# Masked scores: the mask of unlisted keys moves into TensorE's accumulation, and the weights are applied in SBUF

## The chip, the cores and the metric

The kernel runs on one core of one Trainium2 chip. The metric is the device time of one execution in microseconds (us). The kernel before takes 1881.87 us, the median of 3 runs (1881.48 to 1882.13).

The core's engines run side by side, each with an instruction queue of its own: TensorE (PE; its weight loads are PEld), VectorE (DVE), ScalarE (ACT), GpSimd (POOL), and SyncE (SP), which issues most DMA transfers. They wait for each other through semaphores.

## The reference, cut to what matters

Two attention layers over x (2 batches, 1024 tokens, 256 channels, 16 heads of 16) are chained, and a recurrent mixer with a mixture-of-experts feed-forward block follows. The change is in the first of the two:

```python
lam = LAMBDA_MAX * jnp.exp(-ALPHA * u_prev.reshape(Bb))
use_sparse = lam >= SPARSE_THRESHOLD
scores = jnp.einsum('bhqd,bhkd->bhqk', Q, K) * scale
prior_bias = jnp.where(prior_mask[:Ss, :Ss], 0.0, -1.0).astype(x.dtype)
bias = lam[:, None, None, None] * prior_bias[None, None]
dense_out = jnp.einsum('bhqk,bhkd->bhqd', jax.nn.softmax(scores + bias, axis=-1), V)
s_scores = jnp.einsum('bhsd,bhskd->bhsk', Q, K[:, :, idx]) * scale
s_scores = jnp.where(prior_index_mask[:Ss][None, None], s_scores, -jnp.inf)
sparse_out = jnp.einsum('bhsk,bhskd->bhsd', jax.nn.softmax(s_scores, axis=-1), V[:, :, idx])
out = jnp.where(use_sparse[:, None, None, None], sparse_out, dense_out)
```

A query's list of 32 keys may name a key more than once. The kernel therefore computes all scores densely, takes the exponential, and multiplies it with a weight: how often the query lists the key (sparse), or the exponential of the prior's bias (dense).

## The kernel before

**Jobs and units.** The two attentions are sixteen jobs of four heads each (`JOBS`). Jobs 0 to 7 belong to the first attention (`JOBS[n][0] == 0`, the prior one): batch 0, then batch 1, four jobs each. Jobs 8 to 15 are the causal attention. A prior job has 32 units. A unit is one block of 128 keys by 512 queries for two heads: a score tile of 128x1024 f32 in PSUM. `place` gives a unit's half, key block and pair of heads. There are 256 prior units.

**What a unit goes through.** TensorE writes its scores into one of two PSUM tiles (`SC`, the tiles `wide`), two bf16 matmuls of 512 columns (L1867). Then there are two ways, chosen by `to_pool` from the unit's number in its group of eight:

- Units 0, 1, 3, 4, 6 (`POOL_UNITS`, 160 in all): ScalarE copies the scores to SBUF with a Relu that limits them (L1277) and so frees the PSUM tile, takes the exponential from SBUF to SBUF (L1279), and GpSimd multiplies with the weight table (L1085), both its inputs being in SBUF.
- Units 2, 5, 7 (96 in all): ScalarE takes the exponential inside PSUM (L1271), and VectorE takes the minimum with a large number and multiplies with the weights (L1607), reading the scores from PSUM and the weights from SBUF. Only this frees the PSUM tile.

The limits in both ways are there because the scores of unlisted keys can be large: the maximum that is subtracted is taken over listed keys alone. The result lies in one of `N_PROB` = 8 buffers (`prob`). TensorE multiplies it with the values in a "pv" step (L1887), one for each two units, that stands `PV_LAG` = 4 units behind the scores.

**Between the units.** Row maxima of the next jobs run in the same stream: TensorE makes scores into three small PSUM banks (L1842), VectorE adds a bias that removes unlisted keys and takes the maximum (L1554). The stream also holds the projections of the next stage and their split in bf16 parts (ScalarE L1218, L1219 and L1234, GpSimd L1058 and L1062: `second` and `third`), values, normalisation (`num`, `inv`, `times`; GpSimd L1052), and in jobs 3 and 4 the weight tables of batch 1 (`kw` on ScalarE L1263, `kw_sum` on VectorE L1596). One list, `attention_plan`, orders all of it, and each engine takes its own steps from it in that order.

**The start.** Ahead of job 0 GpSimd builds the 16 pieces of batch 0's weight table, each with a scaling (L1073, 128x512 bf16) and a sum (L1077). ScalarE's and VectorE's first writes to `prob` wait until all 16 are there (`prob_vacant`, `weight_p.end`), since the counts of listed keys lie in `prob` until then.

Of the kernel before, what the change touches and what calls it, by code (L numbers as in the profile page):

```python
# [32 lines left out]
N_PROB = 8  # L33
# [20 lines left out]
POOL_UNITS = (0, 1, 3, 4, 6)  # L54
# [401 lines left out]
def build(nc, A, out):  # L456

    with ExitStack() as ctx:
# [151 lines left out]
        count_row = [prob[:, 6, i * HALF:(i + 1) * HALF].bitcast(BF16) for i in range(2)] + [tab[:, i] for i in range(2)]  # L610
# [55 lines left out]
        def columns_of(ap):  # L666
# [6 lines left out]
                    junk=[junk[:].rearrange("p a t -> p (a t)").bitcast(F32)[:, k * D:(k + 1) * D] for k in range(2)]),  # L673
# [52 lines left out]
        weight_p = signal("pool_weight", [(*u[1:], z) for u in of("kw_sum") if u[1] == 0 for z in ("scaled", "sum")])  # L726
# [5 lines left out]
        exp_a = signal("act_exp_wide", [u for u in of("score") if JOBS[u[1]][0] == 0 and not to_pool(*u[1:])])  # L732
        exp2_a = signal("act_exp", [u for u in of("score") if to_pool(*u[1:])])
# [94 lines left out]
        def _(e):  # L828
# [49 lines left out]
            for u in ATT:  # L878
# [42 lines left out]
                elif kind == "late_loads":  # L921
                    fetch_in("wo", wo[:], chunks(A["w_o"]))
                    fetch_in("cf", cf[:], A["const_f32"])
# [111 lines left out]
        def _(e):  # L1035
# [18 lines left out]
            for u in ATT:  # L1054
# [61 lines left out]
        def _(e):  # L1116
# [954 lines left out]
```

## Time and profile before

| | |
|---|---|
| median of 3 runs | 1881.87 us |
| the profiled execution | 1886.38 us |
| its span, first to last instruction | 1884.6 us |
| PE busy | 1585.5 us (84%) |
| DVE busy | 939.7 us (50%) |
| ACT busy | 904.9 us (48%) |
| POOL busy | 590.7 us (31%) |
| mean granted TensorE clock | 0.91 |

The shares are means over stages that differ. The prior jobs take the stretch from 133.44 us (the first score matmul) to 772.91 us (the copy of the last job's result), a third of the span, and in the last 484 us TensorE alone is busy for nearly all of the time. In the windows and timelines each engine's busy time is in us, with the number of instructions; `PEclk` is the share of the full TensorE clock that was granted. In a timeline the number in brackets is the time the engine sat idle before the row, with who ended it.

### The profile page before, as it was taken

What the parts mean: (1) busy time and instruction counts of PE and PEld (TensorE: products, weight loads), DVE (VectorE), ACT (ScalarE), POOL (GpSimd) and SP (SyncE); (2) the same over time, 40 slices, a digit from 0 to 9 for tenths busy, and PEclk for the clock granted to TensorE, in tenths of its full rate; (3) what the DMA queues carried; (4) which work ended last, traced back from release to release, by engine and by line L of the source; (5) the groups of instructions that cost most, each with busy time, mean ns of one, the idle gap of its engine ahead of it and who ended that gap; (6) DMA issues with size and microseconds to landing.
All of it is one profiled execution on the core that took longest, in us unless ns stands there. A gap on an engine that the chain in (4) does not pass through costs nothing.

```text
span 1884.6 us, 19974 instructions
## 1 busy us (share of the span) xinstructions
PE 1585.5 (84%) x7248; PEld 733.1 (39%) x7248; DVE 939.7 (50%) x2075; ACT 904.9 (48%) x1156; POOL 590.7 (31%) x337
## 2 busy tenths in 40 slices
PE   6668777778687777687687979799999999999998
PEld 3322221112222112333233334355565566666655
DVE  7659787888667876444565573234132111111132
ACT  4437888678588888455453546623331111111111
POOL 5566676555568676221000000040000300000051
PEclk9659998787899988898898998899999999999999
DMA  3540212222221201214212101310021002424042
GB/s 103 190 120 26 56 38 66 62 66 70 57 59 46 63 22 45 52 46 119 77 46 69 40 24 59 110 55 1 0 84 50 24 0 81 162 81 162 8 98 44
DMA packets 71517, 121.63 MB, mean 65 GB/s; under 512 B 11048, under 2 KB 49265, under 8 KB 68091
## 3 DMA queue, kind: packets, MB, share of 16 engines
q1 hardware_dynamic: 67771, 113.87, 20.5%
q0 software_dynamic: 3072, 6.03, 1.7%
q8 instruction: 57, 0.93, 0.2%
q10 hardware_dynamic: 576, 0.47, 0.1%
q14 instruction: 41, 0.34, 0.1%
HBM read 85.34 MB, written 36.96 MB: 65 GB/s over the span
## 4 chain that ended last, share of the span: by engine, by line
PE 49%; DMA 9%; ACT 8%; DVE 5%; issue 5%; POOL 2%; SPq 2%; another core or an unknown queue 0%; DVEq 0%; ACTq 0%; POOLq 0%
PE wide L1946 19%; DMA sb_den<-o_raw 5%; PE wide L1958 5%; PE wide L1887 5%; PE wide L1964 5%; PE wide L1867 3%; PE bank L1743 3%; ACT sb_prob L1277 2%; PE bank L1842 2%; POOL sb_prob L1085 1%; DMA parts<-sb_tables 1%; DVE sb_prob L1607 1%; ACT sb_prob L1279 1%; DVE sb_rowmax L1548 1%; PE bank L1735 1%
## 5 line engine op out<-in xcount | busy, mean ns | idle before, releaser
L1085 POOL TENSOR_TENSOR sb_prob<-sb_prob,sb_weight 128x1024 f32<-128x1024 f32 x160 | 377.8, 2371 | 217.6 <-ACT sb_prob L1279 216.7
L1867 PE MATMUL wide<-sb_stack_q,sb_stack_k 99*128 99x512 bf16 (+3 forms) x896 | 282.4, 392 | 105.9 <-DVE sb_prob L1607 80.8
L1842 PE MATMUL bank<-sb_stack_k,sb_stack_q 96*128 96x512 bf16 (+3 forms) x596 | 229.8, 403 | 78.4 <-DVE sb_rowmax L1548 34.8
L1325 ACT ACTIVATE sb_sil<-wide 128x320 f32<-128x320 f32 (+1 forms) x128 | 66.2, 517 | 463.4 <-PE wide L1946 418.8
L1554 DVE CUSTOM_DVE_ANT_0 sb_junk<-bank,sb_bias 128x512 bf16<-128x512 f32 x339 | 225.1, 686 | 72.1 <-PE bank L1842 70.4
L1887 PE MATMUL wide<-sb_prob,sb_v_aug 128*17 128x512 f32 (+3 forms) x1792 | 239.2, 619 | 19.3 <-ACT sb_o_raw L1294 14.0
L1946 PE MATMUL wide<-sb_weight,sb_ffn 128*128 128x512 f32 x512 | 236.1, 605 | 0.0
L1281 ACT ACTIVATE sb_prob<-wide 128x1024 f32<-128x1024 f32 (+1 forms) x192 | 151.6, 810 | 148.9 <-PE wide L1872 78.6
L1277 ACT ACTIVATE sb_prob<-wide,sb_v_aug 128x1024 f32<-128x1024 f32 x160 | 176.5, 1103 | 66.3 <-PE wide L1867 65.6
L1279 ACT ACTIVATE sb_prob<-sb_prob,sb_v_aug 128x1024 f32<-128x1024 f32 x160 | 183.8, 1149 | 5.2
L1699 DVE TENSOR_TENSOR sb_act_s<-sb_sil,wide 128x512 f32<-128x512 f32 x64 | 43.9, 687 | 272.2 <-ACT sb_sil L1325 245.1
L1548 DVE TENSOR_REDUCE sb_rowmax<-bank 128x1 f32<-128x512 f32 (+3 forms) x257 | 136.7, 554 | 79.4 <-PE bank L1845 47.8
L1867 PEld LDWEIGHTS wide<-sb_stack_q,sb_stack_k 99*128 99x128 bf16 x896 | 82.9, 104 | 219.3 <-DVE sb_prob L1607 113.2
L1842 PEld LDWEIGHTS bank<-sb_stack_k,sb_stack_q 96*128 96x128 bf16 x596 | 60.8, 103 | 264.9 <-issue 84.8
L1842 PE MATMUL wide<-sb_stack_k,sb_stack_q 96*128 96x512 bf16 (+3 forms) x300 | 120.9, 403 | 48.2 <-DVE sb_rowmax L1548 16.4
L1946 PE MATMUL wide<-sb_xgT,sb_big 128*128 128x320 f32 x512 | 152.7, 444 | 1.1 <-ACT sb_xgT L1340 1.1
L1946 PEld LDWEIGHTS wide<-sb_weight,sb_ffn 128*128 128x128 f32 x512 | 98.5, 194 | 101.8 <-issue 99.4
L1052 POOL TENSOR_TENSOR sb_o_norm<-sb_o_norm,sb_o_raw 128x1024 f32<-128x1024 f32 x8 | 19.0, 2378 | 379.3 <-DMA sb_o_raw<-inverse 379.3
L1109 POOL DMA_INDIRECT sb_weight<-slots_out,sb_slot_r x32 | 31.3, 977 | 324.3 <-issue 312.9
L1699 DVE TENSOR_TENSOR sb_big<-sb_sil,wide 128x320 f32<-128x320 f32 x64 | 31.2, 487 | 202.0 <-ACT sb_sil L1325 202.0
L1607 DVE SCALAR_TENSOR_TENSOR sb_prob<-wide,sb_weight 128x1024 f32<-128x1024 f32 x96 | 117.1, 1219 | 27.9 <-ACT wide L1271 25.6
L1554 DVE CUSTOM_DVE_ANT_0 sb_junk<-wide,sb_bias 128x512 bf16<-128x512 f32 x173 | 118.6, 686 | 19.7 <-PE wide L1842 19.0
(252 smaller groups left out, 2055.1 us busy)
## 6 DMA issues: line engine op xcount, KB each, us to landing
o_raw<-sb_o_raw SPq DMA_DIRECT2D x32, 256.0 KB, 2.2
sb_big<-rg SPq DMA_DIRECT2D x8, 1024.0 KB, 4.9
sb_big<-ru SPq DMA_DIRECT2D x8, 1024.0 KB, 7.1
sb_big<-rd SPq DMA_DIRECT2D x8, 1024.0 KB, 9.8
sb_stack_q<-parts SPq DMA_DIRECT2D x16, 384.0 KB
sb_stack_k<-parts SPq DMA_DIRECT2D x16, 384.0 KB
parts<-sb_o_norm SPq DMA_DIRECT2D x48, 128.0 KB
sb_stack_q<-parts SPq DMA_DIRECT2D x16, 256.0 KB
```

The lines of the kernel that those rows point to most:

```text
L1085: e.tensor_tensor(p, p, weight_of(*u[1:]), ALU.mult).then_inc(weigh_p.handle, 1)
L1277: e.activation(p, sc, ACT.Relu, scale=-1.0, bias=one).then_inc(SC.empty_sem(u), 1)
L1279: e.activation(p, p, ACT.Exp, scale=-1.0, bias=one).then_inc(exp2_a.handle, 1)
L1281: e.activation(p[:, :, first:HALF], sc[:, :, first:HALF], ACT.Exp).then_inc(SC.empty_sem(u), 1)
L1548: e.tensor_reduce(acc, BK.tile(u)[:, 0:hi - lo], AX.X, ALU.max).then_inc(BK.empty_sem(u), 1)
L1554: e.tensor_tensor_reduce(out=junk[:, i % 2], in0=BK.tile(u)[:], in1=bias[:, qt, lo:hi], scale=1.0, scalar=-3e38, op0=ALU.add, op1=ALU.max, ...
L1607: e.scalar_tensor_tensor(out=p, in0=heads_of(SC.tile(key_)[:]), scalar=HUGE, in1=weight_of(n, v), op0=ALU.min, op1=ALU.mult).then_inc(SC.e ...
L1842: i = e.matmul(bk[:, 0:hi - lo], stack_q[0:ROWS, n % 3, h, qt * P:(qt + 1) * P], stack_k[0:ROWS, n % 3, h, lo:hi], start=True, stop=not diag)
L1867: i = e.matmul(sc[:, j * HALF + first:(j + 1) * HALF], stack_k[0:ROWS_M, n % 3, g, kt * P:(kt + 1) * P], stack_q[0:ROWS_M, n % 3, g, half ...
L1887: i = e.matmul(pv_bank[g * HB:g * HB + DH + 1, first:HALF], v_aug[:, kt, q * QUAD + g, :], prob_tile((n, v))[:, j, first:HALF], start=kt = ...
L1946: m = e.matmul(gu[:, o:o + n], wt[:, c, col * P:(col + 1) * P], src[c], start=(c == 0), stop=(c == DC - 1))
L1958: m = e.matmul(acc[:, t * D:(t + 1) * D], a[:, t * P:(t + 1) * P], wsd[i // ROWS_B][:, i % ROWS_B], start=(i == 0 and t % 2 == 0), stop=Fa ...
```

## The change

Three things happen in the prior jobs.

1. TensorE masks all 256 units. A table `unlisted` (bf16, 1 where a query doesn't list a key) is made by GpSimd, one more step for each of the 16 table pieces. `cut` is a 128x128 diagonal holding -1e30 (0 where the batch is dense). After each score matmul a second one, `cut` by `unlisted`, accumulates into the same PSUM columns. The score step now waits for its piece of `unlisted`.
2. ScalarE has one step for every unit: the exponential from PSUM to SBUF, which frees the PSUM tile.
3. GpSimd weighs units 0, 1, 3, 4, 5, 7 of eight (192 in all), VectorE units 2 and 6 (64 in all), both in SBUF.

To make room, `N_PROB` falls from 8 to 6, the f32 constants are loaded only in part, and a few scratch areas move.

```diff
-N_PROB = 8
+N_PROB = 6
-POOL_UNITS = (0, 1, 3, 4, 6)
+POOL_UNITS = (0, 1, 3, 4, 5, 7)
...
+        unlisted = s1("unlisted", [P, NT, S], BF16)
+        cut = s1("cut", [P, B, P], BF16)
...
         def unit_ready(n, u):
-            return weigh_p.after((n, u)) if to_pool(n, u) else SC.emptied(("score", n, u))
+            if JOBS[n][0]:
+                return SC.emptied(("score", n, u))
+            return weigh_p.after((n, u)) if to_pool(n, u) else weigh_d.after((n, u))
...
+                    e.tensor_scalar(unlisted[:, t, cols], counts[:, t, cols], 0.0, None,
+                                    ALU.is_equal).then_inc(weight_p.handle, 1)
                     e.tensor_scalar(listed_w[t % 2], counts[:, t, cols], fl[3][:, b:b + 1], None,
                                     ALU.mult).then_inc(weight_p.handle, 1)
...
-                    if u in exp_a.value:
-                        e.activation(sc, sc, ACT.Exp).then_inc(exp_a.handle, 1)
-                        continue
                     for mark in prob_vacant(u[1:]):
                         w.wait_ge(mark)
-                    if u in exp2_a.value:
-                        w.wait_ge(const_done.end)
-                        e.activation(p, sc, ACT.Relu, scale=-1.0, bias=one).then_inc(SC.empty_sem(u), 1)
-                        w.wait_ge(SC.emptied(u))
-                        e.activation(p, p, ACT.Exp, scale=-1.0, bias=one).then_inc(exp2_a.handle, 1)
-                    else:
-                        e.activation(p[:, :, first:HALF], sc[:, :, first:HALF], ACT.Exp).then_inc(SC.empty_sem(u), 1)
+                    e.activation(p[:, :, first:HALF], sc[:, :, first:HALF], ACT.Exp).then_inc(SC.empty_sem(u), 1)
...
+            for b in range(B):
+                e.tensor_scalar(cut[:, b], C["ident"], fl[5][:, b:b + 1], None, ALU.mult).then_inc(cut_d.handle, 1)
...
-                    e.scalar_tensor_tensor(out=p, in0=heads_of(SC.tile(key_)[:]), scalar=HUGE, in1=weight_of(n, v),
-                                           op0=ALU.min, op1=ALU.mult).then_inc(SC.empty_sem(key_), 1)
+                    e.scalar_tensor_tensor(out=p, in0=p, scalar=1.0, in1=weight_of(n, v), op0=ALU.mult,
+                                           op1=ALU.mult).then_inc(weigh_d.handle, 1)
...
+                    if not JOBS[n][0]:
+                        w.wait_ge(cut_d.end)
+                        w.wait_ge(weight_p.after((0, kt, half, "cut")))
                     w.wait_ge(SC.vacant(u))
                     for j in range(PAIRS_OF):
                         g = PAIRS_OF * pair + j
                         i = e.matmul(sc[:, j * HALF + first:(j + 1) * HALF],
                                      stack_k[0:ROWS_M, n % 3, g, kt * P:(kt + 1) * P],
                                      stack_q[0:ROWS_M, n % 3, g, half * HALF + first:(half + 1) * HALF],
-                                     start=True, stop=not diag)
+                                     start=True, stop=False if not JOBS[n][0] else not diag)
+                        if not JOBS[n][0]:
+                            i = e.matmul(sc[:, j * HALF:(j + 1) * HALF], cut[:, JOBS[n][1]],
+                                         unlisted[:, kt, half * HALF:(half + 1) * HALF], start=False, stop=True)
```

On TensorE, at the first unit of job 0 (`wide<-sb_stack_q,sb_stack_k` is a score matmul, `bank<-` and `wide<-sb_stack_k,sb_stack_q` are those of the maxima):

```order
 L1800 MATMUL wide<-sb_xT,sb_w_kqv 128x512 x2
-L1867 MATMUL wide<-sb_stack_q,sb_stack_k 128x512 x2
+L1870 MATMUL wide<-sb_stack_q,sb_stack_k 128x512
+L1875 MATMUL wide<-sb_unlisted,sb_cut 128x512
+L1870 MATMUL wide<-sb_stack_q,sb_stack_k 128x512
+L1875 MATMUL wide<-sb_unlisted,sb_cut 128x512
 L1842 MATMUL bank<-sb_stack_k,sb_stack_q 128x512 x2
```

Each unit has four matmuls in the place of two; nothing around them has moved.

On GpSimd before, where job 0 begins, the last piece of the weight table is followed by the weighing of the first units (`sb_prob<-sb_prob,sb_weight`) and a split:

```order
L1073 TENSOR_SCALAR sb_y_prior<-sb_prob,sb_flags 128x512
L1077 TENSOR_TENSOR sb_weight<-sb_weight,sb_y_prior 128x512
L1085 TENSOR_TENSOR sb_prob<-sb_prob,sb_weight 128x1024
L1058 TENSOR_TENSOR sb_o_norm<-sb_o_norm 128x512
L1062 TENSOR_TENSOR sb_tables<-sb_o_norm 128x512
L1085 TENSOR_TENSOR sb_prob<-sb_prob,sb_weight 128x1024 x4
```

And the same place on GpSimd now:

```order
L1078 TENSOR_SCALAR sb_unlisted<-sb_prob 128x512
L1080 TENSOR_SCALAR sb_y_prior<-sb_prob,sb_flags 128x512
L1084 TENSOR_TENSOR sb_weight<-sb_weight,sb_y_prior 128x512
L1092 TENSOR_TENSOR sb_prob<-sb_prob,sb_weight 128x1024
L1063 TENSOR_TENSOR sb_o_norm<-sb_o_norm 128x512
L1067 TENSOR_TENSOR sb_tables<-sb_o_norm 128x512
L1092 TENSOR_TENSOR sb_prob<-sb_prob,sb_weight 128x1024 x5
```

Each of the 16 pieces has one step more, and more weighings stand between the splits.

On VectorE before, the weighing of job 0's first such unit, between a row maximum (two rows, ISA) and the next:

```order
L1554 ISA sb_junk,sb_rowmax<-bank,sb_bias 128x512
L1554 ISA sb_rowmax 128x1
L1607 SCALAR_TENSOR_TENSOR sb_prob<-wide,sb_weight 128x1024
L1554 ISA sb_junk,sb_rowmax<-wide,sb_bias 128x512
L1554 ISA sb_rowmax 128x1
```

And the same place on VectorE now:

```order
L1556 ISA sb_junk,sb_rowmax<-bank,sb_bias 128x512
L1556 ISA sb_rowmax 128x1
L1607 SCALAR_TENSOR_TENSOR sb_prob<-sb_prob,sb_weight 128x1024
L1556 ISA sb_junk,sb_rowmax<-wide,sb_bias 128x512
L1556 ISA sb_rowmax 128x1
```

It stands where it stood, but both its inputs are now in SBUF.

## Rows read from the trace of the kernel before

**Rows 1.** Windows, one for each prior job 0 to 4, 6, 7.

```profile
core 0: us, PE busy (x) PEld busy (x) DVE busy (x) ACT busy (x) POOL busy (x), PEclk, DMA share, GB/s
133.00:220.00 87.00, 72.91 (x330) 23.96 (x330) 76.97 (x202) 63.84 (x67) 56.12 (x28) 0.95 0.09 28
220.00:298.00 78.00, 59.54 (x285) 16.43 (x282) 57.81 (x143) 64.64 (x70) 55.88 (x28) 0.93 0.18 48
298.00:377.00 79.00, 60.45 (x258) 14.29 (x257) 62.48 (x138) 57.69 (x59) 49.88 (x21) 0.78 0.29 76
377.00:465.00 88.00, 67.56 (x274) 16.22 (x273) 76.77 (x171) 68.89 (x73) 48.05 (x20) 0.79 0.22 57
465.00:560.00 95.00, 71.44 (x326) 24.58 (x325) 64.17 (x154) 67.59 (x76) 58.68 (x29) 0.91 0.24 63
...
638.00:707.00 69.00, 52.77 (x278) 13.94 (x275) 50.54 (x112) 57.79 (x59) 49.14 (x21) 0.90 0.18 48
707.00:773.00 66.00, 51.40 (x281) 15.18 (x280) 40.93 (x64) 57.10 (x59) 46.85 (x20) 0.87 0.13 33
```

**Rows 2.** The page's costliest groups: the steps on a prior unit.

```profile
L1085 POOL TENSOR_TENSOR sb_prob<-sb_prob,sb_weight 128x1024 f32<-128x1024 f32 x160 | 377.8, 2371 | 217.6 <-ACT sb_prob L1279 216.7
...
L1277 ACT ACTIVATE sb_prob<-wide,sb_v_aug 128x1024 f32<-128x1024 f32 x160 | 176.5, 1103 | 66.3 <-PE wide L1867 65.6
L1279 ACT ACTIVATE sb_prob<-sb_prob,sb_v_aug 128x1024 f32<-128x1024 f32 x160 | 183.8, 1149 | 5.2
...
L1607 DVE SCALAR_TENSOR_TENSOR sb_prob<-wide,sb_weight 128x1024 f32<-128x1024 f32 x96 | 117.1, 1219 | 27.9 <-ACT wide L1271 25.6
```

**Rows 3.** Groups by line from 250 to 800 us.

```profile
L1271 ACT ACTIVATE wide<-wide 128x1024 f32<-128x1024 f32 x80 | 80.4, 1005 | 23.3 <-PE wide L1867 23.3
...
L1589 DVE TENSOR_SCALAR sb_bias<-sb_tables,sb_flags 128x1024 bf16<-128x1024 bf16 x8 | 9.0, 1122 | 0.0
...
L1058 POOL TENSOR_TENSOR sb_o_norm<-sb_o_norm 128x512 f32<-128x512 f32 x10 | 11.5, 1155 | 0.3 <-ACT sb_o_norm L1219 0.3
```

**Rows 4.** The source line L1867: what ended PE's idle time before it.

```profile
  DVE sb_prob L1607: 194.0, 151
```

**Rows 5.** Timeline of PE, job 5, full clock: the start of a unit's scores and the next matmul.

```profile
650.02 0.60 PE L1867 MATMUL wide<-sb_stack_q,sb_stack_k 99*128 99x512 bf16 x2
...
650.46 0.38 PE L1842 MATMUL bank<-sb_stack_k,sb_stack_q 96*128 96x512 bf16 x1
```

**Rows 6.** Timeline of POOL and DVE around 400 and 416 us, job 3.

```profile
400.74 4.67 POOL L1085 TENSOR_TENSOR sb_prob<-sb_prob,sb_weight 128x1024 f32<-128x1024 f32 x2 [5.26 <-ACT sb_prob L1279]
403.58 2.38 DVE L1596 SCALAR_TENSOR_TENSOR sb_weight<-sb_y_prior,sb_flags,sb_weight 128x512 f32<-128x512 bf16 x1 [1.87 <-ACT sb_weight L1263]
416.31 0.75 DVE L1596 SCALAR_TENSOR_TENSOR sb_weight<-sb_y_prior,sb_flags,sb_weight 128x512 f32<-128x512 bf16 x1
416.55 2.72 POOL L1085 TENSOR_TENSOR sb_prob<-sb_prob,sb_weight 128x1024 f32<-128x1024 f32 x1 [2.99 <-ACT sb_prob L1279]
```

**Rows 7.** Groups by line and form, DVE from 1040 to 1300 us.

```profile
L1436 DVE SCALAR_TENSOR_TENSOR sb_w_kqv<-sb_weight,sb_w_kqv 128x1024 f32<-128x1024 f32 x1 | 1.2, 1219 | 0.0
```

**Rows 8.** Timeline after the end of job 6 (706.6 us).

```profile
706.87 1.06 PE L1867 MATMUL wide<-sb_stack_q,sb_stack_k 99*128 99x512 bf16 x2
...
710.34 4.66 POOL L1085 TENSOR_TENSOR sb_prob<-sb_prob,sb_weight 128x1024 f32<-128x1024 f32 x2 [5.77 <-ACT sb_prob L1279]
```

**Rows 9.** Waits from 450 to 550 us: total, times, longest.

```profile
POOL sb_prob L1085 <- ACT sb_prob L1279: 42.5, 12, 17.6
```

**Rows 10.** Timeline of POOL's table pieces and ACT's first step of job 0.

```profile
75.53 1.15 POOL L1077 TENSOR_TENSOR sb_weight<-sb_weight,sb_y_prior 128x512 f32<-128x512 f32 x1 [4.22 <-ACT sb_weight L1263]
...
104.60 1.56 POOL L1073 TENSOR_SCALAR sb_y_prior<-sb_prob,sb_flags 128x512 bf16<-128x512 bf16 x1
...
126.60 1.15 POOL L1077 TENSOR_TENSOR sb_weight<-sb_weight,sb_y_prior 128x512 f32<-128x512 f32 x1
134.49 1.11 ACT L1277 ACTIVATE sb_prob<-wide,sb_v_aug 128x1024 f32<-128x1024 f32 x1 [12.29 <-PE wide L1867]
```

More of the change, by code:

```diff
@@ L609, in build @@
         lo16, hi16 = (tabs[:, S + i * SPAN:S + (i + 1) * SPAN] for i in range(2))
-        count_row = [prob[:, 6, i * HALF:(i + 1) * HALF].bitcast(BF16) for i in range(2)] + [tab[:, i] for i in range(2)]
+        count_row = [o_raw[:, 1, i * HALF:(i + 1) * HALF].bitcast(BF16) for i in range(2)] + [tab[:, i] for i in range(2)]
         listed_w = [y1[:, i, 0:HALF // 2].bitcast(BF16) for i in range(2)]
@@ L617, in build @@
                        tabs[:, k * HALF:(k + 1) * HALF]) for k in range(2)]
-        idle = [z.bitcast(BF16)[:, k * HALF:(k + 1) * HALF] for z in (prob[:, 4], prob[:, 5], prob[:, 7], y1[:, 0], y1[:, 1])
+        spare = unlisted[:, 0:2].rearrange("p a t -> p (a t)").bitcast(F32)
+        idle = [z.bitcast(BF16)[:, k * HALF:(k + 1) * HALF] for z in (prob[:, 4], prob[:, 5], spare, y1[:, 0], y1[:, 1])
                 for k in range(2 * S // HALF)]
         pairs = [z.bitcast(BF16)[:, k * HALF:(k + 2) * HALF].bitcast(F32) for z, k in
-                 ((prob[:, 4], 0), (prob[:, 5], 0), (prob[:, 7], 0), (y1[:, 0], 0))]
+                 ((prob[:, 4], 0), (prob[:, 5], 0), (spare, 0), (y1[:, 0], 0))]
         rest = [idle[4 * z + k] for z in range(4) for k in (2, 3)] + idle[16:20]
@@ L672, in build @@
         MIX = [dict(ctx=in_y1, gate=in_gate, gated=in_gate, tr=[in_y1, in_gate], soma=in_hT, mod=in_hT, h1=in_gate[0][0:HN],
-                    junk=[junk[:].rearrange("p a t -> p (a t)").bitcast(F32)[:, k * D:(k + 1) * D] for k in range(2)]),
+                    junk=[spare[:, k * D:(k + 1) * D] for k in range(2)]),
                dict(ctx=in_big[0], gated=in_big[1], tr=in_big[2:4], soma=in_big[4], gate=in_big[5], mod=in_big[6],
@@ L725, in build @@
         bias_d = signal("dve_bias", [u[1:] for u in of("kb")])
-        weight_p = signal("pool_weight", [(*u[1:], z) for u in of("kw_sum") if u[1] == 0 for z in ("scaled", "sum")])
+        weight_p = signal("pool_weight", [(*u[1:], z) for u in of("kw_sum") if u[1] == 0 for z in ("cut", "scaled", "sum")])
+        cut_d = signal("dve_cut", range(B))
         weight_d = signal("dve_weight", [u[1:] for u in of("kw_sum") if u[1]])
@@ L731, in build @@
         top_a = signal("act_top", [u for u in of("fin") if u[2] % 2])
-        exp_a = signal("act_exp_wide", [u for u in of("score") if JOBS[u[1]][0] == 0 and not to_pool(*u[1:])])
-        exp2_a = signal("act_exp", [u for u in of("score") if to_pool(*u[1:])])
+        weigh_d = signal("dve_weigh", [u[1:] for u in of("weigh")])
         weigh_p = signal("pool_weigh", [u[1:] for u in of("score") if to_pool(*u[1:])])
@@ L974, in _ @@
                 elif kind == "mixload":
-                    w.wait_ge(SC.emptied(list(exp_a.value)[-1]))
+                    w.wait_ge(weigh_d.end)
                     w.wait_ge(weigh_p.end)
@@ L1080, in _ @@
                     times(u)
-                elif u in exp2_a.value:
+                elif u[0] == "score" and to_pool(*u[1:]):
                     p = prob_tile(u[1:])
-                    w.wait_ge(exp2_a.after(u))
+                    w.wait_ge(SC.emptied(u))
                     w.wait_ge(weight_ready(*u[1:]))
@@ L1384, in _ @@
             e.tensor_scalar(fl[2], fl[2], SPARSE_THRESHOLD, None, ALU.min).then_inc(sf, 1)
+            w.wait_ge(flag_d.after("neg"))
+            w.wait_ge(load["cb"].end)
+            for b in range(B):
+                e.tensor_scalar(cut[:, b], C["ident"], fl[5][:, b:b + 1], None, ALU.mult).then_inc(cut_d.handle, 1)
             sl, sr = ln_d.handle, route_d.handle
```

16 lines of the change are left out of this document (7 added, 9 removed).

## The prediction, on record before the result

> **What bounds the kernel now.** I read the page first: TensorE is busy 84% of the span, but the change touches only jobs 0 to 7, which take 133 to 773 us, 640 us in all. So I cut that stretch into a window for each job [rows 1]. Job 5 (560 to 638 us) is left out of the rows; it repeats job 1: 78 us, with the same busy times within 0.2 us. No engine is full. ScalarE is the fullest in most jobs: 64.6 of 78 us in job 1, 57.8 of 69 in job 6, 57.1 of 66 in job 7, so 83 to 87%. In jobs 0 and 3 it is VectorE: 77.0 of 87 and 76.8 of 88 us. The granted TensorE clock is 0.78 to 0.95.
>
> Then the groups of the steps on a unit [rows 2, 3]. A GpSimd unit costs ScalarE 1.10 + 1.15 us and GpSimd 2.37; a VectorE unit costs ScalarE 1.00 and VectorE 1.22. A job has 20 and 12 of them: 20 x 2.25 + 12 x 1.0 = 57 us of ScalarE. Last, who makes TensorE wait: before score matmuls it sat idle 194 us in 151 waits until VectorE's weighing [rows 4], because that one frees the score tile late, after the exponential and 1.22 us more, and behind row maxima in VectorE's queue. So two things bound a unit: ScalarE's work, and score tiles that are held too long.
>
> **What the change takes away.** ScalarE: 160 x 2.25 + 96 x 1.0 = 457 us become 256 x 1.10 = 282 us [rows 2, 3], so 175 us less; 35 us for a job. It stops being a bound. Score tiles: always free 1.1 us after the scores are there, so the 194 us of waits go. The two are not to be added: they cover each other, and what counts is which engine is the next limit.
>
> **What it adds, and where.**
>
> TensorE: 512 matmuls of 512 columns. Two such matmuls start to start take 650.46 - 650.02 = 0.44 us at the full clock [rows 5], 0.22 each, so 113 us, 14 for a job, and twice that at the half clock. A unit then takes 0.44 + 0.44 of scores, two maxima (0.44) and half a pv step (about 0.5, my estimate from 8 narrow matmuls in about 1 us): 1.8 us, 58 for a job, 72 with the projections of jobs 0 and 4. That is below what follows, though not far.
>
> GpSimd: 192 instead of 160 units at 2.36 to 2.37 us [rows 2]: 76 us more, 57 us for a job.
>
> VectorE: 64 instead of 96 units, and the same operation with both inputs in SBUF takes 1.219 us when GpSimd is quiet [rows 7]. By that alone, 39 us less.
>
> **The disputed cost: VectorE and GpSimd in each other's way.** The old weighing read one input from PSUM and took 1.219 us on the mean beside a busy GpSimd [rows 2]. Operations with two SBUF inputs did not fare so. In job 3 GpSimd weighed two units from 400.74 to 405.41 us. VectorE's sum of two SBUF tables, begun at 403.58, ended at 405.96: 2.38 us instead of the 0.75 that it takes alone [rows 6]. It stood until GpSimd's operation ended, and finished 0.55 us after that. The other way round, at 416.31 VectorE was first, ended at 417.06, and the weighing begun at 416.55 took 2.72 us, ending 2.21 us after VectorE's [rows 6]. So the two take turns, with 0.20 and 0.15 us hidden at the hand-overs.
>
> The Trainium skill says this in "SBUF — State Buffer", section "Who interferes with whom": a VectorE instruction with two SBUF inputs contends with a GpSimd instruction that reads SBUF, and one with at most one SBUF input doesn't. The trace agrees by the 2.38 us and, for the old form, the unchanged 1.219 us. The page has the loser stand for the whole of the other's instruction, with nothing hidden; by that the sum below would be 8 x 2.8 = 22 us higher, 1915 us.
>
> The new weighing has two SBUF inputs and so joins the queue that GpSimd's has. For eight units: 6 x 2.36 + 2 x 1.22 = 16.6 us, less 2 x 0.35 for hand-overs = 15.9. Four such groups: 63.6 us for a job. The old form, 20 x 2.37, was 47. From below: if the large form didn't wait at all, this would be 57 us. From above: nothing hidden, 66.4. I take 63.6, since the rows are of the same kind of instruction.
>
> VectorE also pays: half a weighing of GpSimd, 1.18 us, as a mean wait. Its 8 weighings in a job cost 8 x 2.40 = 19.2 us where 12 x 1.22 = 14.6 were: 4.6 us more.
>
> **The gap between jobs.** A job's last pv stands before the next job's scores, so GpSimd runs dry: 5.77 us after job 6 [rows 8]. The scores there run at the half clock: 1.06 us for the pair instead of 0.60 [rows 5, 8]. After the change the gap loses an exponential (1.15) and gains two matmuls at the half clock (0.88): 5.5 us. Unit 31 is now GpSimd's, at the end of a full queue, so TensorE stands still there at least as long as before, and I see no reason for a better clock. So 63.6 + 5.5 = 69.1 us for a job that GpSimd and VectorE bound. From below 3.9 us: pv 1.0, scores 0.9, exponential 1.1 and 0.9 for other steps and signals, all at the full clock.
>
> **The start.** Each of the 16 table pieces gets one more GpSimd step. From 104.60 to 127.75 us GpSimd made eight pieces without a pause, 2.89 us each [rows 10]. The new step's price isn't in the trace. The nearest row is the scaling of the same shape and type, 1.56 us and some 0.08 to the next; the lower bound is a piece that costs 0.5 in all. I take 1.64. The first piece has room (4.22 us idle before its sum), so from 76.68 us there are 15 pieces of 4.53: the last ends at 144.7 instead of 127.75. ScalarE's first write to `prob`, at 134.49, has to wait for it: 10.3 us late. With 0.5 us a piece it isn't late at all.
>
> **The sum,** by job, us:
>
> - Job 0 (was 87): VectorE had 77.0 busy, now 81.6. It was 88% full; with score tiles out of its way I give it 95%: 86. With the start 96.3. GpSimd's side, 69.1 and 8 split steps of 1.155 [rows 3] = 78.3, is less.
> - Jobs 1 and 5 (78 each): 69.1 + 9.2 = 78.3 each.
> - Job 2 (79): 69.1, one normalisation on GpSimd of the weighing's form (2.4), and 8 bias tables on VectorE that took 9.0 us with waits [rows 3], of which I count half: 76.0.
> - Job 3 (88): VectorE 76.8 + 4.6 = 81.4 at 95%: 85.7.
> - Job 4 (95): 69.1 + 9.2 + 2.4 + 3 for the last table sums = 83.7, and 11.8 of the 17.6 us wait that has other causes [rows 9] and stays: 95.5.
> - Job 6 (69): 69.1 + 2.4 = 71.5. Job 7 (66): 69.1.
>
> Together 650.7 against 640: 10.7 us more. What gains are jobs 2 and 3; the start and jobs 6 and 7 lose. The causal jobs and the tail have no added work and keep their length. Six buffers instead of eight cost nothing: the pv that frees a buffer is ahead of the sixth next unit's scores in TensorE's own queue. The profiled execution took 1886.4 us and so would take 1897.1; it lies 4.5 above the median of the runs, so **1893 us**, 0.6% slower.
>
> **The rivals.**
>
> *Faster: the score tiles' release outweighs all.* TensorE no longer stands, its clock stays full over the gaps (3.9 us), VectorE keeps pace with the shared queue in jobs 0 and 3, and half of the start's delay is hidden. Then 67.5 is the base, and the jobs take 81.7, 76.7, 74.4, 76.5, 93.9, 76.7, 69.9, 67.5: 617, so 23 less, 1859 us. For it: 194 us of waits go [rows 4], and GpSimd has several units queued whenever TensorE is let on. Against: the half clock at the gap, and VectorE at 88% in jobs 0 and 3. It decides if the gap is under 4 us and job 1 under 77.
>
> *Much faster: the large weighing doesn't wait.* 57 us of GpSimd for a job, TensorE 58 to 66, about 7 us less for each job: some 1827 us. Against it stand both pairs in rows 6.
>
> *Clearly slower: three engines at over 90% in one in-order stream.* VectorE, while it stands behind GpSimd, frees no banks for the maxima; TensorE has three and then stands too, falls to the half clock, and takes 2 x 1.8 us for a unit. 5% on 600 us of jobs: 30 more, 1923 us. For it: clocks of 0.78 in jobs 2 and 3 already [rows 1]. Against: TensorE runs up to four units ahead, which covers one such wait of 2.4 + 1.2 us.
>
> **How the numbers follow.** My forecast has 0.43, with 1879 to 1908 as its own range; the faster rival 0.27, the much faster one 0.04, the slower one 0.26. 0.2% is 3.8 us, about what a measurement tells from no change. The forecast's low end reaches into that: 0.12 of its 0.43, and 0.01 of the faster rival's. So faster 0.30, same 0.13, slower 0.57. The range leaves a tenth out on each side: 1860 to 1925 us.
>
> **What the changed profile would show.** ScalarE some 35 us for a job's units, never the reason for long waits. No wait of TensorE's score matmuls for VectorE's weighing. VectorE's weighing at 2 to 2.6 us on the mean instead of 1.22, and GpSimd's above 2.37, by 0.3 or so. GpSimd with VectorE's weighings filling 85% or more of jobs 6 and 7. The first exponential at about 145 us. I am wrong if VectorE's weighing stays near 1.22 us, if the new table step is cheap, or if the granted clock in the jobs rises to 1.0 and the gaps close.

## The result, and the profile after

The changed kernel takes 1911.49 us, the median of 4 runs (1906.48 to 1919.92); the kernel before took 1882.00 beside it, also 4 runs (1881.48 to 1886.10). The ratio is 1.0134, with a 95% interval of 1.0100 to 1.0169: 1.3% slower. Forecast were 1893 us and a range of 1860 to 1925. The sign and the range held. The loss is 29.5 us where the sum gave 10.7, and 1911 us lies above 1879 to 1908, the forecast's own part of the range.

The profiled execution took 1914.72 us (span 1912.9). These groups of its page (busy us, mean ns, then the idle time before them) answer to [rows 2]:

```profile
L1279 ACT ACTIVATE sb_prob<-wide 128x1024 f32<-128x1024 f32 x448 | 412.3, 931 | 405.6 <-PE wide L1875 229.5
L1092 POOL TENSOR_TENSOR sb_prob<-sb_prob,sb_weight 128x1024 f32<-128x1024 f32 x192 | 488.9, 2570 | 106.9 <-ACT sb_prob L1279 106.4
...
L1607 DVE SCALAR_TENSOR_TENSOR sb_prob<-sb_prob,sb_weight 128x1024 f32<-128x1024 f32 x64 | 127.1, 1985 | 8.3 <-ACT sb_prob L1279 8.3
```

VectorE's weighing takes 1.99 us where it took 1.22, and GpSimd's 2.57 where it took 2.37. The first group's 448 include the causal jobs.

Who makes the score matmuls (L1870) wait answers to [rows 4]:

```profile
its engine sat idle before it (us, times) until:
  issue: 64.0, 82
  ACT sb_prob L1279: 47.5, 33
```

VectorE's 194 us are gone. The windows of jobs 1, 3, 6 and 7, with the columns of [rows 1]:

```profile
core 0: us, PE busy (x) PEld busy (x) DVE busy (x) ACT busy (x) POOL busy (x), PEclk, DMA share, GB/s
...
232.00:314.00 82.00, 72.96 (x339) 23.26 (x345) 56.91 (x139) 41.99 (x51) 71.64 (x32) 0.94 0.18 46
...
388.00:474.00 86.00, 68.51 (x332) 21.10 (x337) 79.54 (x166) 45.99 (x53) 61.96 (x24) 0.94 0.23 58
...
656.00:728.00 72.00, 62.18 (x330) 20.38 (x333) 54.28 (x108) 35.22 (x38) 64.89 (x25) 0.95 0.17 46
728.00:797.00 69.00, 61.57 (x343) 21.93 (x349) 46.48 (x60) 35.77 (x39) 62.59 (x24) 0.95 0.13 32
```

ScalarE fell from 78 to 87% of these windows to 49 to 53%. GpSimd now fills 87 to 91% of jobs 1, 6 and 7. In job 3 VectorE, at 79.5 of 86 us, is the fullest, as before.

Here are the jobs' lengths, from 133.44 us and then from one copy of a job's result to the next, and what is left after job 7. "No mask" is experiment 10 and "PSUM" experiment 3, both told of below, and the last row repeats the forecast.

| us | 0 | 1 | 2 | 3 | 4 | 5 | 6 | 7 | sum | rest |
|---|---|---|---|---|---|---|---|---|---|---|
| before | 86.8 | 77.8 | 78.9 | 88.2 | 95.1 | 78.1 | 68.2 | 66.3 | 639.5 | 1111.7 |
| changed | 98.3 | 81.9 | 74.6 | 85.8 | 100.5 | 81.2 | 72.5 | 68.0 | 662.8 | 1116.7 |
| no mask | 90.5 | 81.2 | 76.8 | 85.6 | 101.2 | 81.6 | 68.6 | 66.4 | 651.9 | 1113.7 |
| PSUM | 93.0 | 74.4 | 70.3 | 84.4 | 98.1 | 74.5 | 66.1 | 63.7 | 624.6 | 1106.8 |
| forecast | 96.3 | 78.3 | 76.0 | 85.7 | 95.5 | 78.3 | 71.5 | 69.1 | 650.7 | |

The rest is the same code in all of them. Over the twelve profiles of this study it lies between 1106.8 and 1116.7 us, so its 5.0 us are no effect of the change that I can show. The prior jobs lost 23.3 us, and those are the ones to explain.

### The profile page after: what moved, and what is told of

Same layout as the page of the kernel before. It is cut to its first block, busy times and chain, and to the rows that moved or that the text cites. A ratio compares the mean times of both kernels' runs of the same rounds, so it can differ in the third digit from the quotient of the medians.

```text
span 1912.9 us, 20756 instructions
## 1 busy us (share of the span) xinstructions
PE 1665.4 (87%) x7709; PEld 787.2 (41%) x7760; DVE 951.4 (50%) x2045; ACT 724.8 (38%) x996; POOL 734.6 (38%) x385
## 4 chain that ended last, share of the span: by engine, by line
PE 43%; DMA 6%; DVE 4%; POOL 4%; ACT 3%; issue 2%; SPq 1%; another core or an unknown queue 0%; ACTq 0%; DVEq 0%; POOLq 0%
PE wide L1952 18%; PE wide L1964 5%; PE wide L1970 5%; DMA sb_den<-o_raw 3%; PE wide L1893 3%; POOL sb_prob L1092 3%; PE bank L1743 3%; PE wide L1870 2%; PE bank L1842 1%; DVE sb_rowmax L1550 1%; DMA parts<-sb_tables 1%; ACT sb_prob L1279 1%; DMA sb_stack_k<-parts 1%; PE bank L1735 1%; PE wide L1842 1%
## 5 line engine op out<-in xcount | busy, mean ns | idle before, releaser
L1279 ACT ACTIVATE sb_prob<-wide 128x1024 f32<-128x1024 f32 x448 | 412.3, 931 | 405.6 <-PE wide L1875 229.5
L1092 POOL TENSOR_TENSOR sb_prob<-sb_prob,sb_weight 128x1024 f32<-128x1024 f32 x192 | 488.9, 2570 | 106.9 <-ACT sb_prob L1279 106.4
L1870 PE MATMUL wide<-sb_stack_q,sb_stack_k 99*128 99x512 bf16 (+3 forms) x896 | 310.7, 374 | 36.5 <-ACT sb_prob L1279 19.5
L1842 PE MATMUL bank<-sb_stack_k,sb_stack_q 96*128 96x512 bf16 (+3 forms) x596 | 222.0, 388 | 97.2 <-DVE sb_rowmax L1556 43.2
L1875 PE MATMUL wide<-sb_unlisted,sb_cut 128*128 128x512 bf16 x461 | 180.6, 392 | 0.0
L1842 PE MATMUL wide<-sb_stack_k,sb_stack_q 96*128 96x512 bf16 (+3 forms) x300 | 116.3, 388 | 44.0 <-DVE sb_rowmax L1550 19.8
L1870 PEld LDWEIGHTS wide<-sb_stack_q,sb_stack_k 99*128 99x128 bf16 x896 | 89.0, 101 | 128.3 <-issue 49.6
L1607 DVE SCALAR_TENSOR_TENSOR sb_prob<-sb_prob,sb_weight 128x1024 f32<-128x1024 f32 x64 | 127.1, 1985 | 8.3 <-ACT sb_prob L1279 8.3
L1964 PE MATMUL wide<-sb_ffn,sb_act_s 128*128 128x256 f32 x512 | 120.7, 380 | 1.7 <-DVE sb_act_s L1699 1.7
```

Of the source, the lines that this page charges most:

```text
L1607: e.scalar_tensor_tensor(out=p, in0=p, scalar=1.0, in1=weight_of(n, v), op0=ALU.mult, op1=ALU.mult).then_inc(weigh_d.handle, 1)
L1842: i = e.matmul(bk[:, 0:hi - lo], stack_q[0:ROWS, n % 3, h, qt * P:(qt + 1) * P], stack_k[0:ROWS, n % 3, h, lo:hi], start=True, stop=not diag)
L1870: i = e.matmul(sc[:, j * HALF + first:(j + 1) * HALF], stack_k[0:ROWS_M, n % 3, g, kt * P:(kt + 1) * P], stack_q[0:ROWS_M, n % 3, g, half ...
L1875: i = e.matmul(sc[:, j * HALF:(j + 1) * HALF], cut[:, JOBS[n][1]], unlisted[:, kt, half * HALF:(half + 1) * HALF], start=False, stop=True)
L1964: m = e.matmul(acc[:, t * D:(t + 1) * D], a[:, t * P:(t + 1) * P], wsd[i // ROWS_B][:, i % ROWS_B], start=(i == 0 and t % 2 == 0), stop=Fa ...
```

## The experiments

The expectations are quoted as they stood before each run. Each ratio is to the kernel before, run beside it on the same chip.

**1. Is TensorE a bound? The mask matmuls left out.**

```diff
-                                     start=True, stop=False if not JOBS[n][0] else not diag)
-                        if not JOBS[n][0]:
-                            i = e.matmul(sc[:, j * HALF:(j + 1) * HALF], cut[:, JOBS[n][1]],
-                                         unlisted[:, kt, half * HALF:(half + 1) * HALF], start=False, stop=True)
+                                     start=True, stop=not diag)
```

> The changed kernel without the 512 mask matmuls on TensorE (the scores of unlisted keys stay unmasked; their weight is zero); the tables are still made. Theory A (GpSimd, taking turns with VectorE's weighing, bounds the prior jobs, and TensorE has room): only the gaps between jobs and the first unit get shorter, 0.4 to 0.9 us each, so 5 to 12 us less than the changed kernel: 1900 to 1907 us. Theory B (TensorE's added work bounds them): 60 to 110 us less, 1800 to 1850 us.

Measured: 1908.00 us, ratio 1.0131 (1.0105 to 1.0158), against 1.0134 with them. The 512 matmuls cost nothing that can be told from zero here; the two intervals leave room for some 8 us, so theory A's 5 to 12 us are neither seen nor fully excluded. Theory B's 60 to 110 us are excluded. Jobs 1 to 7 in this run, and below it the same stretch of the changed kernel:

```profile
231.00:794.00 563.00, 436.12 (x1971) 120.63 (x1970) 429.61 (x897) 276.58 (x323) 475.75 (x195) 0.87 0.20 53
231.00:794.00 563.00, 486.59 (x2372) 161.74 (x2412) 422.09 (x897) 281.31 (x322) 469.23 (x195) 0.95 0.20 53
```

Without the mask matmuls TensorE was granted 0.87 of its clock where it had 0.95, so a part of the work left out is given back by slower work on what remains. The rest became idle time: TensorE was idle 127 of 563 us instead of 76. TensorE is not what bounds the changed kernel.

**2. The split five to three, still in SBUF.**

```diff
-POOL_UNITS = (0, 1, 3, 4, 5, 7)
+POOL_UNITS = (0, 1, 3, 4, 6)
```

> The changed kernel with GpSimd on units 0, 1, 3, 4, 6 of eight and VectorE on the other three, the split of the kernel before. Theory A: the shared time of eight units falls from 15.9 to 5 x 2.36 + 3 x 1.22 - 3 x 0.35 = 14.4 us, 6 us for a job, but VectorE gets some 9 us more with its waits, which jobs 0 and 3 don't have room for: 15 to 30 us less than the changed kernel, 1880 to 1896 us. Theory B (TensorE bounds): 1905 to 1917 us, no change. Theory C (VectorE, standing behind GpSimd, is what holds up the stream): slower than the changed kernel, 1920 us or more.

Measured: 1896.41 us, ratio 1.0068 (1.0043 to 1.0093). That is 0.66% less than the changed kernel, some 12 us, a little short of theory A's 15 to 30; theories B and C are out. Job 6 took 66.4 us instead of 72.5, job 7 63.8 instead of 68.0. This fits the shared queue, in which a unit costs 1.2 us if VectorE takes it and 2.4 if GpSimd does, so that giving VectorE one more shortens the whole. Only job 3 got longer, 91.1 instead of 85.8 us, where VectorE was already full.

**3. The same six to two split, with VectorE's two units read from PSUM.** ScalarE leaves their exponentials in the score tile, as before the change; VectorE reads them there.

```diff
+                    if u in exp_a.value:
+                        e.activation(sc, sc, ACT.Exp).then_inc(exp_a.handle, 1)
+                        continue
...
-                    e.scalar_tensor_tensor(out=p, in0=p, scalar=1.0, in1=weight_of(n, v), op0=ALU.mult,
-                                           op1=ALU.mult).then_inc(weigh_d.handle, 1)
+                    e.scalar_tensor_tensor(out=p, in0=heads_of(SC.tile(key_)[:]), scalar=1.0, in1=weight_of(n, v), op0=ALU.mult,
+                                           op1=ALU.mult).then_inc(SC.empty_sem(key_), 1)
```

> The changed kernel, but VectorE's two units of eight go as before: ScalarE's exponential stays in PSUM and VectorE reads it there, so only its weights come from SBUF, and it frees the score tile. Theory A: VectorE's weighing takes 1.22 us instead of 1.99, GpSimd's 2.36 instead of 2.55, 6 us less for a job on GpSimd's side, part of it lost to score tiles held longer: 1875 to 1900 us. Theory D (taking turns costs little, the release of the score tiles is what the change gained): as slow as the changed kernel or slower, 1911 to 1930 us.

Measured: 1872.91 us, ratio 0.9931 (0.9903 to 0.9959). This is 2.0% below the changed kernel's ratio, with the same units on the same engines, and it beats the kernel before. It is also a little below theory A's 1875 to 1900 us. Its page shows the two weighings:

```profile
L1090 POOL TENSOR_TENSOR sb_prob<-sb_prob,sb_weight 128x1024 f32<-128x1024 f32 x192 | 452.8, 2381 | 113.8 <-ACT sb_prob L1280 112.6
...
L1610 DVE SCALAR_TENSOR_TENSOR sb_prob<-wide,sb_weight 128x1024 f32<-128x1024 f32 x64 | 78.0, 1218 | 8.3 <-ACT wide L1276 8.3
```

VectorE's is 49.1 us less in all, GpSimd's 36.1 us less, and the granted clock of jobs 1 and 6 is 0.98 and 1.00 where it was 0.94 and 0.95.

**4. The new table step moved to ScalarE, all 16 pieces.**

```diff
-                    e.tensor_scalar(unlisted[:, t, cols], counts[:, t, cols], 0.0, None,
-                                    ALU.is_equal).then_inc(weight_p.handle, 1)
...
+                        e.activation(unlisted[:, t, cols], counts[:, t, cols], ACT.Relu, scale=-1.0,
+                                     bias=v_aug[:, 0, 0, DH:DH + 1]).then_inc(table_a.handle, 1)
```

> The changed kernel with ScalarE, not GpSimd, making the 16 pieces of the table of unlisted keys, in a stretch where ScalarE mostly waits for loads. Theory A (the table step delays job 0 by its whole length): ScalarE's first exponential at 134 to 136 us instead of 143.4, all later jobs 8 to 9 us earlier: 1900 to 1905 us. Rival: the delay is made up in job 0, since TensorE and VectorE get row maxima done meanwhile: 1908 to 1912 us.

Measured: 1910.86 us, ratio 1.0128 (1.0087 to 1.0169). The first exponential came at 140.83 us, not back at 134 to 136: the 16 steps on ScalarE held up its steps of the maxima's chain (a split of the maxima begun at 117.75 us had begun at 113.49). The time lies in the rival's 1908 to 1912 us, but the delay was only moved, not removed, so the run can't price the start.

**5. Experiment 3 with the split five to three.**

```diff
-POOL_UNITS = (0, 1, 3, 4, 5, 7)
+POOL_UNITS = (0, 1, 3, 4, 6)
```

> As e3_psum (VectorE reads its scores from PSUM), but with the split of the kernel before, GpSimd five units of eight, VectorE three. Theory A (GpSimd's own time is what is left as a bound once VectorE no longer takes turns with it): a job has 47 instead of 57 us of GpSimd, so jobs 6 and 7 shorten by 3 to 8 us each, jobs 0 and 3, full of VectorE work, don't: 1845 to 1868 us against 1873. Rival (score tiles held by VectorE's way set the pace, as in the kernel before): three such units of eight in place of two make it slower, 1873 to 1885 us.

Measured: 1884.17 us, ratio 0.9968 (0.9941 to 0.9995). The rival's mechanism is in the trace. Score matmuls waited for VectorE's weighing (us, times) as this line says, and 44.4 us in experiment 3:

```profile
  DVE sb_prob L1610: 122.1, 127
```

Its price is not clear of the noise, since the ratio is 0.0037 above experiment 3's and the two intervals overlap. What is clear is that with PSUM as the source the third unit on VectorE doesn't gain the 0.66% that it gained in SBUF (experiment 2).

**6. The kernel before with six buffers.**

```diff
-            return heads_of(prob[:, prob_at[key] % N_PROB, :])
+            return heads_of(prob[:, prob_at[key] % 6, :])
...
-            i = prob_at[key] - N_PROB
+            i = prob_at[key] - 6
```

> The kernel before with six buffers of exponentials in use instead of eight, nothing else. The prediction says that six cost nothing, since the pv that frees a buffer stands ahead of the sixth next unit in TensorE's own queue: within 3 us of the kernel before. Rival (part of the loss is the missing slack): 5 us slower or more.

Measured: 1890.10 us beside 1890.23, ratio 0.9994 (0.9971 to 1.0017). The buffers cost nothing that can be measured.

**7. The last unit of each eight on VectorE.**

```diff
-POOL_UNITS = (0, 1, 3, 4, 5, 7)
+POOL_UNITS = (0, 1, 3, 4, 5, 6)
```

> The changed kernel with GpSimd on units 0, 1, 3, 4, 5, 6 and VectorE on 2 and 7, so that a job's last unit is VectorE's as in the kernel before; same load on each engine. If the last unit's place at the end of GpSimd's queue makes the gaps between jobs long, each of eight gaps loses up to 2.4 us: 1892 to 1905 us. If not: 1905 to 1917 us.

Measured: 1912.43 us, ratio 1.0113 (1.0069 to 1.0157), which can't be told from 1.0134. The 1892 to 1905 us that a price of 2.4 us for each gap would give were not reached. That unit 31 stands at the end of GpSimd's full queue costs nothing to speak of.

**8. Experiment 3, and ScalarE makes the first eight table pieces.**

```diff
+                        if not half:
...
+                            e.activation(unlisted[:, t, 0:HALF], counts[:, t, 0:HALF], ACT.Relu, scale=-1.0,
+                                         bias=v_aug[:, 0, 0, DH:DH + 1]).then_inc(table_a.handle, 1)
```

> As e3_psum, and ScalarE makes the first eight pieces of the table of unlisted keys, in the stretch ahead of 100 us where it waits for loads, GpSimd the other eight. GpSimd's chain then ends 8 x 1.49 = 12 us earlier, ahead of the first scores (ready at 134 us): ScalarE's first exponential at about 135 instead of 143 us, 8 us less than e3_psum, 1862 to 1868 us. Rival: as in e4_act, ScalarE's added steps push the maxima's own chain back by as much, and nothing is gained: 1870 to 1876 us.

Measured: 1871.83 us, ratio 0.9904 (0.9870 to 0.9937), the lowest of all, though not apart from experiment 3's 0.9931. But the first exponential stood at 141.68 us (142.55 in experiment 3), not near 135. GpSimd was through with seven pieces by 92 us, and then stood for ScalarE's part of the eighth, and ScalarE for a load:

```profile
101.04 0.72 ACT L1275 ACTIVATE sb_unlisted<-sb_prob,sb_v_aug 128x512 bf16<-128x512 bf16 x1 [15.41 <-DMA sb_y_prior<-priorT]
102.61 1.16 POOL L1084 TENSOR_TENSOR sb_weight<-sb_weight,sb_y_prior 128x512 f32<-128x512 f32 x1 [9.11 <-ACT sb_weight L1277]
```

The changed kernel has the same wait for the load, 15.65 us up to 100.46, but there GpSimd's longer chain hides it. The last eight pieces, with three steps each, follow the wait and still set the start. ScalarE's added steps, the rival's cause, are not what held it.

**9. The mask alone, on the kernel before.** Its two ways, its split and six buffers, plus the table steps and the mask matmuls; only the minimum in VectorE's weighing is left out, which the mask makes needless. Shown against experiment 5, it is ScalarE's two steps put back:

```diff
+                    if u in exp2_a.value:
+                        w.wait_ge(const_done.end)
+                        e.activation(p, sc, ACT.Relu, scale=-1.0, bias=one).then_inc(SC.empty_sem(u), 1)
+                        w.wait_ge(SC.emptied(u))
+                        e.activation(p, p, ACT.Exp, scale=-1.0, bias=one).then_inc(exp2_a.handle, 1)
```

> Part 1 of the change alone: the kernel before (its two ways through ScalarE and VectorE, its five to three split, six buffers), plus the 16 steps that make the mask table and the 512 mask matmuls; the minimum with a large number in VectorE's weighing is left out, since the scores are masked. Theory (the mask costs the start and little else): the first step on prob is about 9 us late, TensorE's added 14 us for a job lie in the 194 us that it waited for VectorE, so job 6 stays at 68 to 70 us and the ratio is 1.004 to 1.008. VectorE weighs at 1.22 us and GpSimd at 2.37. Rival (the mask matmuls come on top, since ScalarE's two ways still bound the jobs and each unit's scores arrive 0.44 us later): 0.44 us for a third or more of the 256 units, so 40 us or more, ratio 1.02 or above, with job 6 at 73 us or more. Second rival (the added columns lift the clock): jobs 2 and 3, at 0.78 before, rise to 0.9 or more and get shorter by 2 us or more each, ratio near 1.00.

Measured: 1912.93 us, ratio 1.0132 (1.0104 to 1.0160), between both theories. The first step on `prob` began at 142.92 us, 8.4 late. Job 0 took 101.0 us instead of 86.8, and jobs 1 to 7 took 567.3 instead of 552.7, 2.1 us each: so where ScalarE still has two steps for a unit the mask matmuls seem to cost something, about a seventh of the 14 us that they add to a job. Job 6, at 71.0 us, lies between the theories too. The second rival came half true: the clock of jobs 2 and 3 rose from 0.78 and 0.79 to 0.96 and 0.94, and they got shorter by 2.7 and 1.3 us, but the other jobs lost more. The waits of score matmuls for VectorE fell only in part, from 194 us [rows 4] to 146.6:

```profile
  DVE sb_prob L1618: 146.6, 133
```

**10. No mask at all in the changed kernel:** neither matmuls nor table steps.

```diff
-                    e.tensor_scalar(unlisted[:, t, cols], counts[:, t, cols], 0.0, None,
-                                    ALU.is_equal).then_inc(weight_p.handle, 1)
...
-                        w.wait_ge(weight_p.after((0, kt, half, "cut")))
```

> The changed kernel without the mask altogether: neither the 512 mask matmuls nor the 16 GpSimd steps that make their table (so unlisted keys are not masked out of large scores). To be read beside the kernel that leaves out the matmuls alone, ratio 1.0131. Theory (the start's delay counts in full): the first exponential is back at 134 to 135 us from 143.4, the jobs after job 0 are as long as in that kernel, and the ratio falls by 8 to 9 us to about 1.008 to 1.009. Rival (job 0 is bound by VectorE's own 77 us and more, and hides most of the delay): the first exponential comes 9 us earlier, but the end of job 0, 231.5 us, by less than 4, and the ratio stays above 1.011.

Measured: 1901.35 us, ratio 1.0073 (1.0046 to 1.0101), against 1.0131 with the table steps (experiment 1). The first exponential was back:

```profile
134.08 1.02 ACT L1277 ACTIVATE sb_prob<-wide 128x1024 f32<-128x1024 f32 x1 [12.38 <-PE wide L1867]
```

Job 0 ended 7.6 us earlier than in experiment 1, and the jobs after it had their lengths within 1 us, but for job 3, which took 1.9 us more. So nearly all of the start's delay counts.

## Why the prediction was right, and where its size was off

**The parts of the loss.** By experiment 10 the start costs about 0.6% (1.0131 less 1.0073), some 11 us, in the profiles 8.5 over the prior jobs (660.4 in experiment 1 less 651.9). Forecast were 10.3. The mask matmuls are the 2.4 us between experiment 1 and the changed kernel (662.8), within the noise. The rest, 0.73% or 14 us, is the exponentials and weighings without any mask; there the profiles have 651.9 less 639.5 = 12.4 us. The forecast had 640.4 without its start, so it gave this part next to nothing. That is the sum's miss.

**The start.** The new table step took 1.49 us where I had taken 1.64 from the scaling. The last sum began at 142.05 us and the first exponential followed:

```profile
142.05 1.16 POOL L1084 TENSOR_TENSOR sb_weight<-sb_weight,sb_y_prior 128x512 f32<-128x512 f32 x1
...
143.36 1.02 ACT L1279 ACTIVATE sb_prob<-wide 128x1024 f32<-128x1024 f32 x1 [20.86 <-issue]
```

It came 8.9 us late; the forecast was 144.8.

**The turn-taking.** It is there as forecast. In job 0:

```profile
149.77 5.63 POOL L1092 TENSOR_TENSOR sb_prob<-sb_prob,sb_weight 128x1024 f32<-128x1024 f32 x2
150.44 2.76 DVE L1607 SCALAR_TENSOR_TENSOR sb_prob<-sb_prob,sb_weight 128x1024 f32<-128x1024 f32 x1 [2.38 <-ACT sb_prob L1279]
```

GpSimd's pair takes 5.63 us instead of 4.67 [rows 6]; VectorE's, begun 0.67 us into it, takes 2.76 instead of 1.22. The page's means are 1.99 us, under my 2.40 (17 of the 64 took under 1.5 us, so hardly waited), and 2.57, which is 0.20 above 2.37 where I had said 0.3 or so. For a job without splits the sum was nearly right: in job 6 GpSimd's 24 weighings with their waits for VectorE take 62.6 us (63.6 forecast for the shared queue), and the whole job 72.5 (71.5). Experiment 3 shows the cause and not only the pattern: with the same split, one input moved to PSUM, both durations are back (1.22 and 2.38) and 2.0% of the time is gone. The Trainium skill's rule ("SBUF — State Buffer", section "Who interferes with whom") is borne out in both directions by these runs, since the PSUM form didn't contend (1.22 us on the mean). Its "whole instruction" is nearly right: 51 of the 64 weighings of VectorE began inside one of GpSimd's steps, and 50 of them ended 1.08 to 1.09 us after that step did, so some 0.14 of the 1.22 us are hidden, and no more.

**What I left out of it.** Other steps with SBUF inputs stand in the same queue. In job 1 (groups by line, 232 to 314 us):

```profile
L1092 POOL TENSOR_TENSOR sb_prob<-sb_prob,sb_weight 128x1024 f32<-128x1024 f32 x24 | 59.0, 2480 | 9.4 <-ACT sb_prob L1279 9.4
L1067 POOL TENSOR_TENSOR sb_tables<-sb_o_norm 128x512 bf16<-128x512 f32 x4 | 6.6, 1642 | 0.0
L1063 POOL TENSOR_TENSOR sb_o_norm<-sb_o_norm 128x512 f32<-128x512 f32 x4 | 6.6, 1640 | 0.0
```

The eight splits took 13.2 us, not 9.2: four of them met a weighing of VectorE and took 2.13 us. But they took turns in the place of weighings, which came to 59.0 us and not 63.6. GpSimd's 72.2 us are what I had (72.8).

**The step that failed.** "Jobs 1 and 5 (78 each): 69.1 + 9.2 = 78.3 each", and the like sum of job 4: they take GpSimd's steps and one gap of 5.5 us as the whole job. GpSimd stood idle 9.4 us in job 1, in four waits, of which 5.4 are the gap, 9.9 in job 5 (forecast 5.5 both), and 27.6 in job 4, where I had 5.5 + 11.8. All are waits for exponentials. The three extra ones of job 1 have different causes. At 252.64 us (1.90 us idle) the scores were late, made at the half clock (0.43 us start to start), and at 256.75 us (0.51) a projection stood ahead of them. At 292.34 us the scores were there, but ScalarE had stood 3.34 us for a split on GpSimd, itself delayed by a turn:

```profile
290.72 0.63 ACT L1241 ACTIVATE sb_o_norm<-sb_o_norm 128x512 bf16<-128x512 f32 x1 [3.34 <-POOL sb_o_norm L1063]
292.34 2.36 POOL L1092 TENSOR_TENSOR sb_prob<-sb_prob,sb_weight 128x1024 f32<-128x1024 f32 x1 [1.65 <-ACT sb_prob L1279]
```

ScalarE's waits of this kind come to 7.1 us in job 1 of the changed kernel and 2.9 in that of the kernel before. Projections and splits thus cost more than their GpSimd time, and the profile of before said so already: job 1 was 9.5 us longer than job 6, where my terms make it 6.8. In the changed kernel it is 9.4, in experiment 3, without VectorE's turns, 8.3. Jobs 2, 3, 6 and 7, which hold no splits, came within 1.4 us of the forecast; jobs 1, 4 and 5 were under-sized by 3.6, 5.0 and 2.9. No experiment takes these waits away one by one, so their shares in the 3 to 5 us are read from the trace and not shown. They aren't the mask matmuls: without them (experiment 1) the three took 81.2, 101.8 and 81.4.

**Job 0** was under-sized by 2.0, and by a wrong rule: "VectorE at 95%". It was busy 75.6 of 99 us. In experiment 10, without the delayed start, job 0 took 90.5 us where my 86 stood, and VectorE was busy for 81% of it. The miss of 4.5 us was partly covered by luck, since the start cost job 0 only 7.5 to 7.8 us of my 10.3. What rules job 0 instead wasn't isolated.

**TensorE, "below what follows, though not far".** Right for the changed kernel (experiment 1). The mask isn't free as such: alone on the old code it costs 1.3%, as much as the whole change (experiment 9), half of that in job 0, where the late start is. ScalarE's relief then brings 1.6% (0.9968 in experiment 5). The move to weighing in SBUF takes 1.0% of it away at the same split (1.0068, experiment 2), and the sixth unit on GpSimd the other 0.7%. Four ratios put that side by side:

| split | weighed from SBUF | from PSUM |
|---|---|---|
| 6 to 2 | 1.0134 | 0.9931 |
| 5 to 3 | 1.0068 | 0.9968 |

The step from 0.9931 to 0.9968 is within the noise, the others are not.

**The rivals.** The faster one had the waits for VectorE right: they went. But "its clock stays full over the gaps" didn't happen, and both of its signs failed: the gap after job 6 is 5.34 us (5.5 forecast, under 4 wanted), and job 1 took 81.9 us (under 77 wanted).

```profile
731.58 12.57 POOL L1092 TENSOR_TENSOR sb_prob<-sb_prob,sb_weight 128x1024 f32<-128x1024 f32 x5 [5.34 <-ACT sb_prob L1279]
```

The much faster one fell with the means of the page. The clearly slower one is right in its first half. VectorE, standing behind GpSimd, does free the banks of the maxima later, and TensorE waits for it; over the prior jobs (total, times, longest):

```profile
PE bank L1842 <- DVE sb_rowmax L1556: 34.8, 25, 10.7
```

The same wait was 18.6 us in the kernel before and 18.1 in experiment 3, where VectorE takes no turns in its weighings. Its second half, TensorE at the half clock, is wrong: the granted clock rose, from 0.78 and 0.79 in jobs 2 and 3 to 0.97 and 0.94, and those jobs got shorter by 4.3 and 2.4 us, as forecast. The measured 1911 us lies between the forecast and this rival's 1923. Six buffers cost nothing (experiment 6).

## What to carry to other kernels

When two engines share one elementwise job over SBUF, give the faster one an input in PSUM if the producer can leave it there: the same work cost 2.0% less of this kernel. A relief of one engine is worth only what the next shared resource leaves; sum that resource over both engines, and add the other steps that use it too. And check a sum of terms against a difference that the old profile already has (here job 1 less job 6), since idle time that a kind of step brings along stands in no group of instructions.

## What the runs showed of the hardware

- More TensorE work went with a higher clock: over 231 to 794 us the granted clock was 0.95 with the mask matmuls and 0.87 without them, at the same time within the interval. On the old code it was 0.87 in jobs 1 to 7 without them and 0.96 with them (experiment 9).
- The turn-taking doesn't look at size, and it was there before the change: VectorE's sum of 128x32 tables (L1577), with both inputs in SBUF in every kernel, took 1.62 us in job 1 of the changed kernel. In experiment 3 it took 0.27 in job 1 and 2.35 in job 2, and a like step took 0.20 in job 7 with GpSimd idle.
- It isn't always one turn each. In job 7 of experiment 3 three weighings of GpSimd, the first already running, went ahead of that step, back to back until 736.02 us. What lets GpSimd pass twice is open.

```profile
730.45 5.64 DVE L1578 SCALAR_TENSOR_TENSOR sb_mneg<-sb_mneg,sb_mpart 128x32 f32<-128x32 f32 x1 [0.32 <-ACT sb_mpart L1247]
```

- The same VectorE instruction on the same amount of data took 1.22 us with one input in PSUM beside a busy GpSimd, and 1.21 to 3.39 us with both in SBUF (mean 1.99).
